# Inverse norms of projected rows: a power on GpSimd, or a square root on ScalarE and a reciprocal on VectorE

## What is computed

```python
q = _l2norm(_silu(h @ Wq)); k = _l2norm(_silu(h @ Wk)); v = _silu(h @ Wv)   # 8 heads of 64
_l2norm = lambda x: x * rsqrt(sum(x * x, axis=-1) + 1e-06)
beta, g = gates(h)                  # per row and head; two of four experts per row
S = S * exp(g); S = S + k (v - k S) beta; o = (q * 64**-0.5) S    # a scan over the rows of each expert
out = x + (rms_norm(o) * weight * silu(h @ Wg)) @ Wo
```

## Time and profile before

| | us |
|---|---|
| median of 3 runs | 957.79 (955.58 to 961.64) |
| the profiled execution, its own time | 954.94 |
| its span in the profile | 953.1 |

### The profile page before, as it was taken

How to read it: one execution, slowest core, us unless ns; L and a number is a source line. 1 busy time by engine, 2 the same in 40 slices (tenths; PEclk the granted TensorE clock), 3 DMA queues, 4 the chain that set the end, 5 groups by cost and what they waited for, 6 DMA issues and landing times.

```text
span 953.1 us, 24758 instructions
## 1 busy us (share of the span) xinstructions
PE 869.4 (91%) x10668; PEld 561.1 (59%) x10668; DVE 636.9 (67%) x1308; ACT 258.9 (27%) x462; POOL 386.7 (41%) x313
## 2 busy tenths in 40 slices
PE   3989999999999899999999967899999999998598
PEld 2444443445666444444444447888899899887343
DVE  7999999968887323223436446777777687774284
ACT  1221113201222000015113114444344444443331
POOL 6221100001111300000589837776677777661572
PEclk9999999999999899999999989999999999999989
DMA  9500000120000330000036754444445444521452
GB/s 242 162 0 1 1 1 1 44 65 1 1 1 2 104 139 0 1 0 1 4 84 264 284 190 112 108 131 121 123 118 135 112 131 117 128 67 40 122 152 67
DMA packets 74964, 80.54 MB, mean 84 GB/s; under 512 B 34452, under 2 KB 57670, under 8 KB 74853
## 3 DMA queue, kind: packets, MB, share of 16 engines
q1 hardware_dynamic: 69733, 57.78, 22.2%
q0 software_dynamic: 5120, 21.14, 6.2%
HBM read 54.44 MB, written 24.39 MB: 83 GB/s over the span
## 4 chain that ended last, share of the span: by engine, by line
PE 55%; DVE 25%; POOL 10%; issue 6%; DMA 2%; ACT 1%; SPq 1%; DVEq 0%; POOLq 0%
PE bank L765 9%; PE bank L834 8%; PE bank L859 5%; PE bank L568 4%; PE bank L1022 4%; DVE rows L1490 3%; PE bank L554 3%; POOL nrm L1320 3%; DVE rows L1492 3%; PE bank L756 3%; POOL qkv_slots L1325 3%; DVE rows L1619 2%; DVE tB L1878 2%; PE bank L850 2%; POOL gb_slots L1315 2%
## 5 line engine op out<-in xcount | busy, mean ns | idle before, releaser
L756 PE MATMUL bank<-W,xT 128*128 128x512 f32 x296 | 128.3, 593 | 0.0
L756 PEld LDWEIGHTS bank<-W,xT 128*128 128x128 f32 x296 | 56.0, 190 | 69.9 <-issue 69.7
L765 PE MATMUL bank<-hs,big 125*125 125x512 f32 x200 | 86.6, 593 | 0.0
L1301 POOL TENSOR_TENSOR big<-big,ident_sb 125x125 f32<-125x125 f32 x10 | 11.4, 1142 | 173.8 <-ACT big L1085 173.8
L532 PE MATMUL bank<-W,xT 128*125 128x512 f32 x160 | 77.9, 600 | 0.0
L765 PEld LDWEIGHTS bank<-hs,big 125*125 125x125 f32 x200 | 37.3, 188 | 47.7 <-issue 47.5
L554 PEld LDWEIGHTS bank<-rows 128*126 128x126 f16 x360 | 43.5, 135 | 34.7 <-issue 24.2
L1625 DVE TENSOR_SCALAR rows<-iota_sb,tC 128x625 f16<-128x625 f16 x180 | 56.2, 378 | 10.5 <-PE bank L554 10.5
L554 PE MATMUL bank<-rows 128*126 128x313 f16 x360 | 58.9, 299 | 4.2 <-DVE rows L1625 4.1
L834 PE MATMUL bank<-big 64*64 64x64 f32 x1600 | 56.7, 218 | 1.9 <-issue 1.1
L1490 DVE TENSOR_SCALAR rows<-iota_sb,gbp 125x180 f16<-125x180 f16 x160 | 56.3, 352 | 0.0
(11 more groups left out here) (328 smaller groups left out, 1980.6 us busy)
## 6 DMA issues: line engine op xcount, KB each, us to landing
big<-qkv_slots SPq DMA_DIRECT2D x40, 256.0 KB, 3.4
rows<-step_rows SPq DMA_DIRECT2D x40, 128.0 KB, 3.1
rows<-gam_rows SPq DMA_DIRECT2D x40, 128.0 KB, 3.4
big<-qkv_slots SPq DMA_DIRECT2D x80, 64.0 KB, 2.7
big<-qkv_slots SPq DMA_DIRECT2D x40, 128.0 KB, 3.0
o_slots<-big SPq DMA_DIRECT2D x40, 128.0 KB, 2.8
x_all<-in_x SPq DMA_DIRECT2D x10, 224.0 KB
out<-tC SPq DMA_DIRECT2D x10, 224.0 KB
```

The lines of the kernel that those rows point to most:

```text
L756: last = mm(bank[:, b0, :], xT[:, k, t * P:t * P + 128], W[:, w, k, :], start=(k == 0), stop=(k == KC - 1))
L765: last = mm(bank[0:P, t % 2, :], cnt[:, s, t * P:(t + 1) * P], hs[:, s, :], start=(s == 0), stop=(s == NT - 1))
```

## The change

ScalarE takes the square root of tile `t`'s sums in place, as soon as they are there, behind the three Silus of tile `t` (for tiles 0 and 1: behind tile 1 and the gate of tile 0). It now counts `rn_done`. VectorE takes the reciprocal in place at the head of `unit_rows` and waits for it there. GpSimd's powers go; it scatters tile after tile.

```diff
+            def row_norms(t):
+                act.wait_ge(S["ss_done"], t + 1)
+                A(nrm[:, t % 4, :], nrm[:, t % 4, :], ACT.Sqrt).then_inc(S["rn_done"], 1)
+
             act.wait_ge(S["consts_loaded"], 32)
             A(pairs16[:, :], level0T, ACT.Copy).then_inc(S["ln_table"], 1)
             for w in range(3):
                 feature_rows(1, w)
             feature_rows(0, 3)
+            for t in range(2):
+                row_norms(t)
             for t in range(2, NT):
                 for w in range(3):
                     feature_rows(t, w)
+                row_norms(t)
                 if t == DECAY_AT:
                     decays()
...
-            def inverse_norm(t):
-                pool.wait_ge(S["ss_done"], t + 1)
-                G.tensor_tensor(nrm[:, t % 4, :], nrm[:, t % 4, :], phalf[:, 0:2 * H], ALU.pow).then_inc(S["rn_done"], 1)
-
...
             for t in range(NT):
                 gates_out(t)
-            inverse_norm(0)
             for t in range(NT):
-                if t + 1 < NT:
-                    inverse_norm(t + 1)
                 rows_out(t)
...
                 dve.wait_ge(S["rn_done"], t + 1)
+                step(V.reciprocal(nrm[:, b, :], nrm[:, b, :]))
                 V.scalar_tensor_tensor(tt3(qk[:, 0:D]), tt3(qk[:, 0:D]), DH ** -0.5, bc(nrm[:, b, 0:H], DH), ALU.mult, ALU.mult)
```

## The result

The changed kernel takes 978.42 us in the median of 4 runs (975.34 to 983.81), the kernel before 956.68 in four runs (954.83 to 961.64; the 957.79 above is the median of three of them): ratio 1.022, 95% interval 1.0185 to 1.0255. That is 21.7 us slower; 18.6 were forecast, with 976.4 us as the time.

What follows compares the result with a forecast made beforehand. TensorE's projection stream was taken to bound the stage. Second-place delay 16.35 us (containing the first 5.25) plus 2.7 clock minus 0.4 gain gave 18.6 us, so 957.79 + 18.6 = 976.4 us; range 964 to 981.

Steps and rivals of the forecast that it cites:

- TensorE's stream sets the stage; freeing GpSimd is worth 0.4 us: Projection stage: TensorE is busy 118.92 of 119.00 us, so removing GpSimd's ten powers gains at most 0.4 us.
- First place: Tiles 0 and 1: ScalarE's roots wait for VectorE's second sum, delaying tile 2's first Silu and TensorE by 5.25 us.
- Second place: Tile 4: its root waits for VectorE, held at gate copies until the gate rows load; TensorE 16.35 us late.
- L + 6.2 - 493.55: Delay of TensorE's tile 6: gate load's landing plus 6.2 us of following work, less its old start; 16.35 us.
- L: Time the gate load lands: taken as 503.7 us, bounds 493.0 and 503.7.
- The load ends last: DMA engines: the gate load lands after six row scatters, at about 503.7 us; late gate rows given chance 0.58.
- at one for one the rows all pass first: DMA engines: one scattered row passes per load run, so 48 queued rows go before the load's 320 runs per engine.
- The first delay is contained in the second: TensorE's stream: the 16.35 us behind tile 4 already contains the first 5.25 us.
- Clock, 2.7 us once: TensorE's granted clock falls after its long pause, adding 2.7 us once; 0 if it holds, 5.4 if it falls twice.
- Table loads are hidden, and a switch costs only its load: ScalarE: 2.8 us per tile hidden in steady state, each load 1.28 us; costlier-switch rival 977.7 us, chance 0.08.
- The reciprocals cost nothing: VectorE: ten added reciprocals, 6.6 us within 57 us idle, cost 0 on the path, at most 0.7 us.
- Behind tile 4 nothing is late: Stage after tile 4: Silus, sums and scatters move with TensorE's stream, adding no further delay.

Runs made afterwards that it cites:

- run without roots: Kernel before without GpSimd's powers, reciprocal on VectorE, no square root anywhere; ratio to the kernel before 1.0014.
- loads alone: Kernel before plus ten square roots on ScalarE that read a constant and wait for nothing; ratio to the kernel before 0.9978.
- both waits mended: Changed kernel with gate copies behind tile 5 and each root one tile later on ScalarE; ratio to the kernel before 1.0007.
- waits alone: Changed kernel with a copy in place of the square root on ScalarE; ratio to the kernel before 1.0169, median 978.32 us.
- gates later: Changed kernel with VectorE's gate copies behind tile 5 instead of tile 2; ratio to the kernel before 1.0073.
- rows waiting: Changed kernel with GpSimd's row scatters held back until the gate rows are loaded; ratio to the kernel before 1.0067.
- first roots later: Changed kernel with only the roots of tiles 0 and 1 moved behind tile 2; ratio to the kernel before 1.0215.

## Why the prediction was right, point by point

The mechanism and the time both came out: TensorE held twice by Silus behind late sums, 18.6 us forecast, 21.5 found in the stage.

- *TensorE's stream sets the stage; freeing GpSimd is worth 0.4 us.* Right: 0.44 us in the trace, nothing that could be measured in the run without roots.
- *First place, 5.25 us.* Right: 5.24.
- *Second place, L + 6.2 - 493.55.* The form is right: the load landed at 489.68 + 15.55 = 505.2 by the chain, and 505.2 + 6.2 = 511.4, where TensorE went on at 511.32. L itself was 1.5 us later than the 503.7 taken, 0.9 of it because the scatters and the load went out 0.9 later than reckoned (first scatter 487.67 against 486.8), and the stream began 1.2 us sooner than before; together these are most of the 2.9 us by which the stage's 21.5 exceed the 18.6.

```profile
489.68 15.55 DMA gbp<-gb_slots
```

- *The load ends last.* Right in its result, and the scatters as the cause are shown. The picture behind it, "at one for one the rows all pass first", is right only in part: 1,916 of the runs went through from 491 to 493, when the first scatters had mostly passed, and from 493 to 502 it was about three runs for two rows. The sum didn't need the full picture: the engines were filled up to 502, and nearly half of the load was still left when the rows ended, so it landed when all the work was done. The Trainium skill's rule of turns by packets ("DMA: Bandwidth & Descriptors", "Queues, rings and completion order") fits these counts; no run here measured the turns of one engine by themselves.
- *The first delay is contained in the second.* Right, by the run that took the first away and won nothing.
- *Clock, 2.7 us once.* Right in size: the slow matmuls cost 3.0 us behind the first pause and 2.9 behind the second, and the first lies ahead of the second pause and is contained in it.
- *Table loads are hidden, and a switch costs only its load.* Right: 1.28 us, the next instruction 0.01 to 0.02 behind it, and the run with loads alone was not slower. Their count was wrong, 17 more and not twenty, which the sum doesn't use. The 2.66 us that the Trainium skill gives ("ScalarE: Activation LUTs", "What ACT_TABLE_LOAD costs") don't show in this trace.
- *The reciprocals cost nothing.* Nothing of theirs appears on the path; the run with both waits mended contains all ten.
- *Behind tile 4 nothing is late.* Right: the next 96 matmuls take 41.36 us, as before.
- *From the start of the recurrence the same length as before.* Not confirmed in the traces, and the one point left open. From that start to the end, the five traces with a pause of TensorE in the stage take 399.9 to 403.8 us, the four without (the kernel before, the loads alone, both mended, no root) 394.9 to 398.1. The groups don't overlap, but each is one execution, and no run took the link apart. The five lie 0.3 to 2.7 us above the medians of their kernels, the four from the median to 3.1 below. The medians show no such link: in the five (the change, waits alone, gates later, rows waiting, first roots later) they exceed the kernel before, as run beside each, by 21.7, 17.5, 7.4, 7.2 and 21.7 us, the stages alone by 21.5, 18.9, 8.0, 7.3 and 19.2, the same sum within 1 us.

The 18.6 us were 3.1 too small against the medians' 21.7. The stage has nearly all of these in what is listed above: the later landing (1.5), the earlier start of the stream (1.2) and the clock (0.2).

## What to carry to other kernels

Moving an operation onto an idle engine also moves its wait into that engine's order: before asking what the operation costs, ask what is queued behind it and when its operand really arrives. Here the operations alone cost nothing that can be measured; two waits did. And freeing an engine releases what stood behind it: a delay on GpSimd had kept six large scatters away from a small load that, two engines on, TensorE depends on. Where a wait could not be avoided, putting it later in the queue was enough: the roots by one tile, the gate copies by three.

## What was unexpected

A load of 2 x 160 KB in short runs took 4.2 us alone and up to 15.5 us beside six row scatters, near the forecast; but with its reader moved away it took still longer, 21.7 and 23.6 us, while further scatters came in, since nothing held the later tiles back. The clock fell even behind the 3.79 us pause of the run with waits alone (72 matmuls in 32.86 us against 31.1 at the pace of the 96 in 41.45; granted 0.63 from 466.4 to 470), but not behind 0.55 us. Nor is its price fixed: behind the first pause, 5.24 us in the changed kernel and 5.21 with the scatters held back, the same 72 matmuls took 33.99 and 32.66 us.
